# A fused conditioning, attention and expert kernel: all adds on VectorE, and a reordered start

## The reference

```python
def cond_ref(x, cond):                      # two projections, scaled and shifted by cond
    w_down = down_project * (cond @ down_gamma) + cond @ down_beta      # 256 x 64, one per batch
    w_up = up_project * (cond @ up_gamma) + cond @ up_beta              # 64 x 256, one per batch
    return relu(x @ w_down) @ w_up + x

def attn_ref(h):                            # 8 heads, DEPTH 5
    paths = sigmoid(h @ Wp + bp)            # 5 numbers per token and head
    agree = pq * pk + (1 - pq) * (1 - pk)   # for query q and key k
    sim = cumprod(agree, -1).sum(-1) / 5, masked to keys at or before the query
    return softmax(sim) @ (h @ Wv) @ Wo

def cond2_ref(x, cond):                     # a weight of rank 30, made from cond
    U = (cond @ W_dec + b_dec).reshape(4, 257, 30)
    return x @ (U[:, :-1] @ V) + U[:, -1] @ V

def ffn_ref(y):                             # one of 8 experts per token, by argmax
    return y + (expert_w[argmax(y @ gate_w.T)] applied to y)

x = x + attn_ref(cond_ref(x, cond))
x = x + ffn_ref(cond2_ref(x, cond))
```

## Time and profile before

| | us |
|---|---|
| median of 3 runs | 148.36 (147.6 to 149.44) |
| the profiled execution | 148.48 |
| its span in the trace | 146.8 |
| PE busy | 135.0 (92%) |
| DVE busy | 99.5 (68%) |
| ACT busy | 59.3 (40%) |
| POOL busy | 50.4 (34%) |

### The profile page before, as it was taken

One profiled execution on the slowest core, in us unless ns is written; L12 is line 12 of the kernel. 1 busy time (PEld: TensorE's weight loads), 2 busy tenths in 40 slices (PEclk: granted clock), 3 DMA queues, 4 the chain that ended last, 5 costly groups with the idle time before them and its releaser, 6 DMA issues.

```text
span 146.8 us, 4941 instructions
## 1 busy us (share of the span) xinstructions
PE 135.0 (92%) x2190; PEld 85.6 (58%) x2190; DVE 99.5 (68%) x180; ACT 59.3 (40%) x73; POOL 50.4 (34%) x71
## 2 busy tenths in 40 slices
PE   5688879999989999998899999999899998999992
PEld 5464456654636685665556675657467674657651
DVE  1434557685995866799956859697567967884531
ACT  3011645655664406473531475265316364310010
POOL 7300029006063560660446615602566660300000
PEclk9999999999999999999999999999999999999999
DMA  4899999800022000000110100001101010111212
GB/s 142 277 464 420 384 367 349 308 17 0 2 36 36 4 0 4 0 4 2 40 36 4 38 4 0 26 14 40 36 4 36 4 36 4 38 38 38 71 40 71
DMA packets 7381, 12.62 MB, mean 86 GB/s; under 512 B 1552, under 2 KB 5808, under 8 KB 7232
## 3 DMA queue, kind: packets, MB, share of 16 engines
q1 hardware_dynamic: 7264, 12.26, 23.6%
q0 software_dynamic: 96, 0.05, 0.3%
HBM read 10.09 MB, written 2.22 MB: 84 GB/s over the span
## 4 chain that ended last, share of the span: by engine, by line
PE 58%; DVE 19%; DMA 8%; issue 6%; ACT 2%; POOL 2%; SPq 2%; DVEq 0%; ACTq 0%; POOLq 0%
PE work L666 32%; PE s_ps L666 12%; PE c_ps L666 10%; DMA x_t<-in_x_tr 4%; DVE tiles L606 3%; DMA u_scratch<-u_row 3%; DVE rden L495 2%; DVE tiles L609 2%; ACT prob L434 2%; DMA u_raw<-u_scratch 2%; POOL zo L418 2%; PE work L857 2%; DVE zo L637 1%; PE work L797 1%; DVE feat L656 1%
## 5 line engine op out<-in xcount | busy, mean ns | idle before, releaser
L434 ACT ACTIVATE prob<-s_ps 128x1536 f32<-128x1536 f32 (+1 forms) x24 | 38.2, 1594 | 35.4 <-PE s_ps L666 35.4
L399 POOL TENSOR_SCALAR_AFFINE_SELECT prob<-prob 128x1024 f32<-128x1024 f32 x16 | 18.4, 1150 | 66.3 <-ACT prob L434 66.3
L495 DVE RECIPROCAL rden<-c_ps 128x256 f32<-128x256 f32 x16 | 28.1, 1755 | 6.6 <-PE c_ps L666 6.5
L666 PE MATMUL s_ps<-phi_t 32*128 32x256 f32 (+1 forms) x384 | 24.1, 365 | 0.9 <-DVE phi_t L557 0.6
L666 PEld LDWEIGHTS s_ps<-phi_t 32*128 32x128 f32 x384 | 17.3, 184 | 11.2 <-issue 8.3
L666 PE MATMUL c_ps<-prob,v_sb 128*32 128x256 f32 (+1 forms) x384 | 22.1, 348 | 0.0
L411 POOL TENSOR_TENSOR short<-prob 128x512 f32<-128x512 f32 x15 | 21.0, 1402 | 1.3
L666 PE MATMUL work<-ctx_t,mix_sb 128*32 128x256 f32 x256 | 17.0, 381 | 0.4 <-ACT zo_t L477 0.2
L666 PE MATMUL work<-zo_t,gexp 128*32 128x256 f32 x256 | 16.9, 379 | 0.0
L666 PEld LDWEIGHTS c_ps<-prob,v_sb 128*32 128x32 f32 x384 | 10.7, 109 | 8.8 <-issue 2.8
L666 PE MATMUL work<-w_vl,h_t 128*32 128x296 f32 x208 | 15.1, 415 | 0.4 <-DVE h_t L540 0.4
(11 more groups left out here) (110 smaller groups left out, 149.3 us busy)
## 6 DMA issues: line engine op xcount, KB each, us to landing
wdec<-in_W_dec SPq DMA_DIRECT2D x1, 3855.0 KB, 17.0
x_t<-in_x_tr SPq DMA_DIRECT2D x4, 512.0 KB, 8.1
ex_t<-in_expert_tr SPq DMA_DIRECT2D x1, 2048.0 KB, 23.2
out_x<-x_t SPq DMA_DIRECT2D x16, 128.0 KB, 1.7
mix_sb<-in_mix SPq DMA_DIRECT2D x1, 904.0 KB, 18.7
lift_sb<-in_lift SPq DMA_DIRECT2D x1, 384.0 KB, 3.0
w_vl<-in_vl SPq DMA_DIRECT2D x1, 296.0 KB, 6.2
first_sb<-in_first SPq DMA_DIRECT2D x1, 144.0 KB, 2.2
```

What stands on the lines that cost most here:

```text
L399: nc.gpsimd.affine_select(out=tri, in_=tri, compare_op=ALU.is_ge, fill=0.0, base=0, pattern=[[0, HG], [0, 2], [1, P]], channel_multiplier= ...
L434: nc.scalar.activation(prob[:, p % 2, :, 0:width(p)], s_ps[:, :, 0:width(p)], ACT.Exp).then_inc(exped, 1)
L495: link(nc.vector.reciprocal(rden[:], c_ps[m % 2][:, CW:2 * CW]))
L666: return nc.tensor.matmul(o, w, r, start=start, stop=stop, skip_group_check=True)
```

## The change

- Loads: the up matrices (`lift`) are issued by ScalarE's queue, once the identity is ready, and no longer by SyncE ahead of `x`.
- `WARM` is 4.
- Prologue: `gdn` of batches 1 to 3 stands before `gup` of batch 0, and both before `down` of batch 0; the second `tanh` comes before `down` of batch 1; `ugT` comes from behind `scores(2)` to ahead of `scores(0)`; `up(1, 0)` from behind `scores(1)` to behind `scores(0)`.
- `w_lift` is a step of its own (`wlift`), behind `scores(2)`. `Q` comes from behind `context(4)` to behind `scores(2)`; `phi` of the second head group from behind `scores` of the last pair but one to one pair later; the transpose `lift` of batch 3 from the first batch to the second.
- ScalarE scales every `phi` of batches 1 to 3, so two products of 512 columns move there from VectorE.
- GpSimd adds nothing for the denominators any more. VectorE makes `short` for the pairs 0 and 1 of a batch (8 adds of 512 elements). A closing pair is summed by VectorE in two adds of 1024 and 512 elements straight from `prob`.
- Every add but the first stands right behind `context` of the pair before, its opening ones too.

```diff
-WARM = 8
+WARM = 4
 def mixing(p):
-    return pair(p)[1][3] and p < ALL - 1
+    return pair(p)[1][1] == 0
 def scaler(s):
-    if s[3] == ALL_T:
-        return "scalar" if s[2] == 1 or s[1] == 1 else "vector"
-    return "scalar" if s[2] == 0 and s[3] == FIRST else "vector"
+    return "scalar" if s[3] == ALL_T or s[2] == 0 and s[3] == FIRST else "vector"
-PROLOGUE = [("gdn", (0,)), ("gup", 0), ("down", 0), ("gdn", (1, 2, 3)), ("up", 0, 0), ("up", 0, 1), ("gup", 1),
-            ("VL", 0, 0), ("VL", 0, 1), *features(0, FIRST), ("feat", 0, FIRST), ("VL", 0, 2), ("VL", 0, 3), ("bias", 0, SECOND),
-            ("down", 1), ("phi", 0, 0, FIRST), ("phi", 0, 1, FIRST), ("tanh", 0, SECOND), ("scores", 0),
-            ("feat", 0, SECOND), ("phi", 0, 0, SECOND), ("phi", 0, 1, SECOND)]
+PROLOGUE = [("gdn", (0,)), ("gdn", (1, 2, 3)), ("gup", 0), ("down", 0), ("up", 0, 0), ("up", 0, 1), ("gup", 1),
+            ("VL", 0, 0), ("VL", 0, 1), *features(0, FIRST), ("feat", 0, FIRST), ("VL", 0, 2), ("VL", 0, 3),
+            *features(0, SECOND), ("down", 1), ("phi", 0, 0, FIRST), ("phi", 0, 1, FIRST), ("ugT",), ("scores", 0),
+            ("feat", 0, SECOND), ("up", 1, 0), ("phi", 0, 0, SECOND), ("phi", 0, 1, SECOND)]
 def after_scores(b):
-        gaps[0] += [("up", n1, 0), ("up", n1, 1)]
+        gaps[0] += [("up", n1, 0)] if b else []
+        gaps[0] += [("up", n1, 1)]
         gaps[3] += [("feat", n1, ALL_T)]
-        gaps[4] += [("phi", n1, 0, ALL_T), ("phi", n1, 1, ALL_T)]
+        gaps[4] += [("phi", n1, 0, ALL_T)]
+        gaps[5] += [("phi", n1, 1, ALL_T)]
     if b == 0:
-        gaps[1] += [("ugT",), ("U", 1)]
+        gaps[1] += [("wlift",), ("Q",), ("U", 1)]
...
-        gaps[5] += [("lift", 3), ("Uadd",)]
+        gaps[5] += [("Uadd",)]
 def after_context(b):
-        gaps[4] += [("G", 0), ("ubT",), ("Q",)]
+        gaps[4] += [("G", 0), ("ubT",)]
...
+        gaps[2] += [("lift", 3)] if b == 1 else []
 # ORDER
-        if opening(_p):
-            ORDER += [("add", _p)]
+        if _p == 0:
+            ORDER += [("add", 0)]
         ORDER += [("context", _p)]
         ORDER += _c
-        if _p + 1 < ALL and long(_p + 1) and not opening(_p + 1):
+        if _p + 1 < ALL and (long(_p + 1) or mixing(_p + 1)):
             ORDER += [("add", _p + 1)]
 # SyncE
-            sp.dma_start(lift_sb[:], lift).then_inc(ld_lift, 16)
 # ScalarE
+            act.wait_ge(ident_ready, 1)
+            act.dma_start(lift_sb[:], lift).then_inc(ld_lift, 16)
 # GpSimd, behind the mask
-                    if mixing(p):
...
-                        nc.gpsimd.tensor_tensor(short[:, mixes(p) % 2], both[:, :, 0, P:CW], both[:, :, 1, 0:P], ALU.add
-                                                ).then_inc(mixed, 1)
 # VectorE
                     acc = tiles[:, chunk(p) % 2]
+                    if mixing(p):
+                        dve.wait_ge(masked, masks(p))
+                        if mixes(p) > 2:
+                            dve.wait_ge(summed, SHORT[mixes(p) - 3] + 1)
+                        nc.vector.tensor_tensor(short[:, mixes(p) % 2], both[:, :, 0, P:CW], both[:, :, 1, 0:P], ALU.add
+                                                ).then_inc(mixed, 1)
+                        continue
...
-                        nc.vector.tensor_tensor(acc[:, :, 0:P], acc[:, :, 0:P], both[:, :, 0, 0:P], ALU.add
-                                                ).then_inc(added, 1)
-                        dve.wait_ge(mixed, mixes(p))
-                        nc.vector.tensor_tensor(acc[:, :, P:CW], acc[:, :, P:CW], short[:, mixes(p) % 2], ALU.add
-                                                ).then_inc(added, 1)
+                        nc.vector.tensor_tensor(acc, acc, both[:, :, 0, :], ALU.add).then_inc(added, 1)
+                        dve.wait_ge(added, adds(p) - 1)
+                        nc.vector.tensor_tensor(acc[:, :, P:CW], acc[:, :, P:CW], both[:, :, 1, 0:P], ALU.add
+                                                ).then_inc(added, 1)
```

More of the change, by code:

```diff
@@ L100, in scaler @@
 def scaler(s):
-    if s[3] == ALL_T:
-        return "scalar" if s[2] == 1 or s[1] == 1 else "vector"
-    return "scalar" if s[2] == 0 and s[3] == FIRST else "vector"
+    return "scalar" if s[3] == ALL_T or s[2] == 0 and s[3] == FIRST else "vector"
 def features(b, ts):
     return [("bias", b, ts), ("tanh", b, ts)]
-PROLOGUE = [("gdn", (0,)), ("gup", 0), ("down", 0), ("gdn", (1, 2, 3)), ("up", 0, 0), ("up", 0, 1), ("gup", 1),
-            ("VL", 0, 0), ("VL", 0, 1), *features(0, FIRST), ("feat", 0, FIRST), ("VL", 0, 2), ("VL", 0, 3), ("bias", 0, SECOND),
-            ("down", 1), ("phi", 0, 0, FIRST), ("phi", 0, 1, FIRST), ("tanh", 0, SECOND), ("scores", 0),
-            ("feat", 0, SECOND), ("phi", 0, 0, SECOND), ("phi", 0, 1, SECOND)]
-EARLY_BANK = {("gdn", (0,)): 0, ("gup", 0): 1, ("down", 0): 2, ("gdn", (1, 2, 3)): 3, ("up", 0, 0): 4, ("up", 0, 1): 5,
-              ("gup", 1): 0, ("VL", 0, 0): 1, ("VL", 0, 1): 2, ("VL", 0, 2): 4, ("VL", 0, 3): 5, ("down", 1): 0,
-              ("phi", 0, 0, FIRST): 1, ("phi", 0, 1, FIRST): 2}
+PROLOGUE = [("gdn", (0,)), ("gdn", (1, 2, 3)), ("gup", 0), ("down", 0), ("up", 0, 0), ("up", 0, 1), ("gup", 1),
+            ("VL", 0, 0), ("VL", 0, 1), *features(0, FIRST), ("feat", 0, FIRST), ("VL", 0, 2), ("VL", 0, 3),
+            *features(0, SECOND), ("down", 1), ("phi", 0, 0, FIRST), ("phi", 0, 1, FIRST), ("ugT",), ("scores", 0),
+            ("feat", 0, SECOND), ("up", 1, 0), ("phi", 0, 0, SECOND), ("phi", 0, 1, SECOND)]
+EARLY_BANK = {("gdn", (0,)): 0, ("gdn", (1, 2, 3)): 3, ("gup", 0): 1, ("down", 0): 2, ("up", 0, 0): 4, ("up", 0, 1): 5,
+              ("gup", 1): 0, ("VL", 0, 0): 1, ("VL", 0, 1): 2, ("VL", 0, 2): 4, ("VL", 0, 3): 5, ("down", 1): 3,
+              ("phi", 0, 0, FIRST): 1, ("phi", 0, 1, FIRST): 2, ("ugT",): 0}
 def after_scores(b):
@@ L189 @@
           ("out", B - 1, 1), ("zoT", B - 1, 1), ("out", B - 1, 2), ("out", B - 1, 3)]
-NO_BANK = ("scores", "context", "add", "bias", "tanh", "feat", "Uadd", "zo")
+NO_BANK = ("scores", "context", "add", "bias", "tanh", "feat", "Uadd", "zo", "wlift")
 EARLY = 6
@@ L401, in _ @@
                                             ).then_inc(masked, 1)
-                    both = prob[:, p % 2].rearrange("p h (s q) -> p h s q", s=2)
-                    pool.wait_ge(masked, masks(p))
-                    if mixing(p):
[L405 to L410, removed]
-                        nc.gpsimd.tensor_tensor(short[:, mixes(p) % 2], both[:, :, 0, P:CW], both[:, :, 1, 0:P], ALU.add
-                                                ).then_inc(mixed, 1)
                 elif s[0] == "zo" and s[1] < B - 1:
@@ L520, in _ @@
                                           ).then_inc(empty(s), 1)
-                    done(dve, s)
+                elif kind == "wlift":
+                    done(dve, ("ugT",))
                     dve.wait_ge(ld_mix, 16)
```

## The result

The changed kernel took 151.91 us in the median of 4 runs (150.78 to 154.12), against 147.98 for the kernel before. The ratio is 1.021, interval 1.0145 to 1.0275: 1.5 to 2.8% slower, where 146.6 had been forecast. On another occasion the same kernel gave 1.013 (1.0014 to 1.024).

A forecast was written before the change was run, and what follows sets the result against it. TensorE was taken as the bound, busy 135.0 of 146.8 us. Loads 0.1, first batch 0.5 and adds 1.2 sum to 1.8 us: 148.36 - 1.8 = 146.6; own range 145.2 to 147.6, 8 in 10 within 144.5 to 148.7.

The forecast's parts named there:

- Part 1, the loads: Start: x and lift both land at about 6.7, down(0) starts at 7.6; gain 0.1, range gain 1.2 to loss 1.7.
- the bound of 6.4: Loads, estimate from below: lift lands at 4.6, so x alone decides, landing at 6.4.
- The second estimate: Loads, by the skill page's shared DMA engines: x gains some 0.5 us, lift loses some 2; sum stays near the forecast.
- the far bound: Loads, estimate from above: the other queue's 6.8 us from issue to landing gives 8.4, and down(0) at 9.4.
- the value nearest to the row of the same 1040 KB: Loads, the estimate taken: both transfers land at about 6.7 (7.57 before), down(0) at 7.6, a gain of 0.1.
- rival C: Start: lift is late, down(0) at 9.4, 1.8 us later than forecast; 148.4, no change; chance 0.12.
- Part 2: First products: halved warm-up starts gdn at 3.4, not 4.7, worth nothing; moving gdn(1, 2, 3) gives 0.8 us.
- The gain of 0.8: First VL: h_t starts at 10.0 instead of 10.8, as gdn(1, 2, 3) no longer stands between down(0) and up.
- Part 3, the first batch: First batch: ugT, VectorE's work and the trip of u eat most of the lead; 0.5 us saved.
- Rival B: VectorE takes over: no slack behind normalise in four of eight places, 2.8 us replace the gain; 149.4; chance 0.11.
- Part 4, the closing adds: Batches 1 to 3: stalls removed, new ones of 0.4 at last pairs of batches 1 and 2; 1.2 us saved.
- "0.42" of the forecast: Closing pair after its mask: 1.95 us instead of 2.37, each 0.42 better where the mask ends the wait.

The follow-up runs named there:

- WARM 16: The changed kernel with WARM = 16 and nothing else changed; 151.29 us, all four runs between 150.89 and 151.63.
- the reorder alone: The changed kernel with the adds of before, lift on SyncE ahead of x, and WARM 8; 147.02 us, ratio 0.994 to the kernel before.
- the adds alone: The kernel before with only the adds and their places changed; loads, prologue and WARM as before; 150.66 us, ratio 1.014.

## Why the prediction was wrong

*Part 1, the loads: wrong for both transfers.* Both were put at 6.7 us. `x` landed at 5.0 (3.8 us from its issue at 1.2), below even the bound of 6.4; `lift` landed at 7.5 to 7.9, 5.9 to 6.4 us from its issue, within its bounds and near the other queue's 6.8. The second estimate, `x` some 0.5 earlier and `lift` some 2 later, had both signs; measured were 2.6 and 3.2 to 3.7. `down(0)` started at 9.97, past the 9.4 of the far bound. The step that failed is "the value nearest to the row of the same 1040 KB": that row told when the last of the bytes land, and the up matrices now were the last. `gup(0)` in front of `down(0)` then made the last transfer gate the first use of the first one. It was seen as rival C and priced at 148.4, no change.

*Part 2, "That gain ends in the wait for the loads, so it is nothing".* In the profiled runs this failed most. The product costs were taken from rows at full rate, and the trace of before had the half rate in view: 0.21 us for a warm-up record, 0.16 for the same shape later; the eight records that WARM 4 leaves take 0.26 each. What the warm-up bought was not asked. With half of it, and a longer wait behind it, `gup(0)`, `down(0)`, `up` and `gup(1)` ran at half rate, some 4 us of products that took 8. Of the 4.3 us lost before `VL(0, 0)`, WARM 16 shows how much the rate makes: `down(0)` to `VL(0, 0)` is 4.2 us there (9.52 to 13.76), 6.55 in the changed kernel (9.97 to 16.52). That is 2.3 for the rate, and `down(0)` is 2.3 later than before, 1.0 of it `gup(0)` at half rate and the rest the load.

The gain of 0.8 from `gdn` leaving its old place was also too large. The kernel with WARM 16 needs 4.24 us from `down(0)` to `VL(0, 0)` and the one before 4.47: 0.2. The first `h_t` starts 1.1 us after `up`, not 0.7; in the trace of before `h_t` waited for `up` and for `w_dn`, both ending at 10.8, and only one was counted.

*Part 3, the first batch.* The forecast let normalise(0) start 0.2 earlier. From `VL(0, 0)` it took 12.0 us before, was forecast at about 12.7, took 12.8 with the reorder alone, and 14.2 in the kernel with old loads, WARM 8 and all adds on VectorE, the stall of 1.22 among it. So the reorder's share was right in size, but two of its terms were missing: behind the wait of 0.58 that the forecast names, the kernel before had two more, 0.64 and 0.30, and all three shrink to one of 0.4; and `up(1, 0)`, called "work done earlier", costs 1.1 by standing alone. The step that failed: "the add of pair 0 stands on VectorE behind one `h_t`", counted as 0.69 of VectorE. The cost was not the length of `h_t` but the idle wait for `up(1, 1)` in front of it, and the mask that had begun by then. The eight short adds were costed "at nothing". The first, in its place, cost 1.4 us (149.12 against 147.71), the other seven together up to 1.2 by the medians (147.71 against 146.5), of which the profiles show 0.6, all of it in pair 6. For the other six "at nothing" held. Rival B, four adds of 0.69 or 2.8 us, had the sign and nearly the size; what it had wrong is the place, since it was two adds, each in front of or behind an operation that something waits for.

*Part 4, the closing adds: the stalls right, their cause in part wrong.* The row of 1.22 for 1024 elements alone held (1.220), the stalls at pair 3 and in the last batch are gone, and the new one at the last pair came, 0.17 for the 0.4 said. 1.2 us were forecast for this part and 0.7 were seen after `up(2, 0)`, where the transposes of `lift(3)`, 0.4 us moved in from the first batch, had not been charged. But the reorder alone, with GpSimd's adds, has 1.3 us there, and the stalls of 0.37 and 0.62 that were credited to the adds are gone in it. What the closing adds themselves removed is the 0.51 of the last batch, for two new stalls of 0.17, and 0.4 in the first batch, the "0.42" of the forecast. And "nothing of GpSimd is beside it" missed the masks: in the first batch the opening add stretched a mask to 1.97, up to 0.64 of the stall of 0.92. That `up(2, 0)` waits for the trip of u and for `gexp` held: 0.3 to 0.9 us of idle time there in all the reordered kernels.

Summed from medians: the new load order about +2.9 (151.91 against 149.0 with it undone), the reorder -1.0, the adds +2.1 to the reordered kernel (149.12 against 147.02). That makes 4.0, and 3.9 was measured; the pieces were timed on different occasions, and the changed kernel's own median was 152.47 on another, so the agreement is in part luck. Without the half rate the sum is smaller: with WARM 8 the runs at a granted clock of 1.0 stand at 150.2 and 150.3 with the new loads and at 149.0 in the middle with the old, so the late load itself is worth about 1.2 us. What the medians of the changed kernel lie above 150.2, 1.7 to 2.3 us, is then likely the half rate's part; it was not measured by itself.

## What to carry to other kernels

A load moved to another queue is not faster for it: ask which transfer lands last afterwards, and keep its first user out of the way of what is already there. Before a warm-up is cut or a wait in the start lengthened, ask at what rate the products behind it will run, by comparing equal products in the trace. When an operation is moved onto an engine with a strict order, price the longest wait of the operation in front of it, not its length, and look for what begins on the other engine in the meantime. When a product is moved alone, look whether it ran beside its neighbour: two halves that took 1.14 us together took 1.13 each when apart.

## What the runs showed of the hardware that had not been expected

An add of two halves of `prob` or `tiles` on VectorE and a mask on GpSimd that overlap: the one that starts second is stretched, by nearly the overlap. The add that began 0.12 us after a mask took 1.53 for 0.69, 0.84 more where the mask had 0.98 to go; the mask that began 0.2 after an add took 1.97 for 1.10, 0.87 more where the add had 1.02 to go. In each case the first kept its length. Not every VectorE operation does this: in the changed kernel the masks beside the reciprocal and beside `h_t` kept their 1.10. The cause inside the chip was not tried.

When TensorE's rate rises at the start is not fixed by the number of warm-up products alone. In the five kernels with old loads, the reorder and WARM 8, whose starts are the same steps, the six records of `gdn(1, 2, 3)` took 0.83, 0.84, 0.99, 1.03 and 1.49 us in the profiles; 1.49 is also what they took in the changed kernel at half rate.

TensorE's rate can also fall once in the middle of a run. In the profile of the adds alone the granted clock over 20 to 24 us was 0.58 (columns: stretch, sum, busy time of each engine, granted clock, DMA share, GB/s), and `up` took 2.08 for about 1.1:

```profile
20.00:24.00 4.00, 3.69 (x30) 2.42 (x32) 0.84 (x3) 1.84 (x2) 1.58 (x2) 0.58 1.08 355
```

```profile
21.88 2.08 PE L661 MATMUL work<-act_t,w_up 64*128 64x256 f32 x8
```

Ahead of it TensorE had been idle three times, 0.58, 0.64 and 0.30 us. The profile of the changed kernel with the load on SyncE has such a fall too, at another place, behind two idle stretches of 0.74:

```profile
56.22 0.68 PE L663 MATMUL c_ps<-prob,ones 128*32 128x128 f32 x8
```

The same eight records take 0.40 in the profile of before. Both runs have a mean granted clock of 0.989 and are the longest of their ten (151.79 and 151.85). Of the kernel before, 4 runs in 25 read 0.988 or 0.989 as well, and they took 149.53 to 150.54 where the median is 148.22. Why the clock fell in those runs and not in others with the same gaps stays open.
